# A transformer block with a mixture of experts: the router of the first 1536 tokens moved into the attention, the last 512 tokens prepared beside 16 expert tiles

## The reference

```python
h = _layernorm(x, axis=-1) * (1 + ca) + sa
x = x + ga * attention(h)         # 16 query heads of 64, 4 key/value heads, rotary, causal, fp32
h = _layernorm(x, axis=-1) * (1 + cb) + sb
x = x + gb * experts(h)           # 8 experts of 128 -> 512 -> 128, two per token

def experts(x):
    router_logits = x @ gate
    routing_weights, selected = jax.lax.top_k(router_logits, 2)
    routing_weights = jax.nn.softmax(routing_weights, axis=-1)
    out_of_expert = (silu(x @ w1[e]) * (x @ w3[e])) @ w2[e]
    return sum over the two selected experts of routing_weight * out_of_expert
```

## Time and profile before

| | us |
|---|---|
| three runs without a profile: median (lowest to highest) | 1238.19 (1237.99 to 1241.21) |
| the profiled execution, its own time | 1241.08 |
| its span | 1238.9 |
| TensorE busy in the span | 1088.2 (88%) |
| DVE busy | 854.7 (69%) |
| ScalarE busy | 540.0 (44%) |
| POOL busy | 603.7 (49%) |

### The profile page before, as it was taken

The page is one execution under the profiler, slowest core; times in us unless marked ns, Lnnn a source line. Parts: engine busy times, 40 slices in busy tenths (PEclk is TensorE's granted clock), DMA queues, the critical chain, the costliest instruction groups (busy, mean ns, idle before and its releaser), DMA issues.

```text
span 1238.9 us, 16497 instructions
## 1 busy us (share of the span) xinstructions
PE 1088.2 (88%) x5698; PEld 657.5 (53%) x5698; DVE 854.7 (69%) x1680; ACT 540.0 (44%) x1149; POOL 603.7 (49%) x649
## 2 busy tenths in 40 slices
PE   3589999999999999999999999999999973039993
PEld 2355555554565655455655554555565533029993
DVE  3647878777778786868787867778786658305553
ACT  2344544544445445454454545454544433014441
POOL 2733645645346565346446735445545233734441
PEclk9689999999999999999999999999999996559997
DMA  8000000000000000000000000000000006121104
GB/s 233 1 1 1 1 2 1 1 1 1 1 1 1 1 1 1 1 1 2 1 1 1 1 1 1 1 1 1 1 1 1 1 1 203 46 60 51 48 23 117
DMA packets 31921, 25.08 MB, mean 20 GB/s; under 512 B 8432, under 2 KB 26992, under 8 KB 31840
## 3 DMA queue, kind: packets, MB, share of 16 engines
q1 hardware_dynamic: 22272, 16.94, 4.6%
q0 software_dynamic: 2272, 4.72, 1.1%
q10 hardware_dynamic: 7296, 2.36, 0.8%
HBM read 15.62 MB, written 8.40 MB: 19 GB/s over the span
## 4 chain that ended last, share of the span: by engine, by line
PE 74%; DVE 12%; POOL 5%; issue 3%; DMA 2%; ACT 2%; ACTq 1%; SPq 0%; POOLq 0%; DVEq 0%
PE PS L1205 19%; PE PS L1159 12%; PE PS L1187 11%; PE PS L1189 9%; PE PS L1270 4%; POOL sent L614 3%; PE PS L1135 3%; PE PS L1224 3%; PE PS L1289 2%; DVE part_max L885 2%; PE PS L1172 2%; PE PS L1142 2%; PE PS L1215 2%; DVE full L901 2%; PE PS L1162 1%
## 5 line engine op out<-in xcount | busy, mean ns | idle before, releaser
L885 DVE TENSOR_REDUCE part_max<-PS 128x1 f32<-128x512 f32 (+2 forms) x576 | 340.3, 618 | 134.0 <-PE PS L1159 111.8
L692 ACT ACTIVATE full<-PS 128x512 f32<-128x512 f32 x384 | 223.5, 599 | 198.2 <-PE PS L1189 186.1
L1187 PE MATMUL PS<-rounded 128*128 128x512 f32 (+3 forms) x640 | 271.9, 425 | 5.9 <-ACT diag L701 2.4
L1159 PE MATMUL PS<-rounded 128*128 128x512 f32 (+3 forms) x640 | 250.1, 417 | 2.4 <-DVE V L866 1.3
L561 POOL TENSOR_TENSOR full<-full 128x512 f32<-128x512 f32 x128 | 164.4, 1315 | 155.5 <-PE PS L1205 154.5
L1189 PE MATMUL PS<-rounded 128*128 128x512 f32 (+3 forms) x640 | 233.5, 365 | 0.0
L701 ACT ACTIVATE diag<-PS 128x512 f32<-128x512 f32 (+3 forms) x256 | 111.4, 441 | 216.3 <-PE PS L1192 186.3
L589 POOL TENSOR_TENSOR rot_cos<-qkv_sb,cos_sb 128x320 f32<-128x320 f32 x64 | 60.3, 942 | 276.3 <-DVE qkv_sb L863 274.0
L1159 PEld LDWEIGHTS PS<-rounded 128*128 128x128 f32 x640 | 119.8, 193 | 139.0 <-DVE part_max L885 62.2
L1205 PE MATMUL PS<-full,V 128*64 128x512 f32 x768 | 190.0, 605 | 0.0
L1187 PEld LDWEIGHTS PS<-rounded 128*128 128x128 f32 x640 | 122.9, 192 | 80.8 <-ACT diag L701 27.0
(11 more groups left out here) (153 smaller groups left out, 1481.9 us busy)
## 6 DMA issues: line engine op xcount, KB each, us to landing
full<-in_L_ffn_experts_w_dram SPq DMA_DIRECT2D x16, 256.0 KB, 6.9
sent<-full SPq DMA_DIRECT2D x1, 2574.0 KB, 18.9
full<-sent SPq DMA_DIRECT2D x9, 264.0 KB, 2.9
full<-made SPq DMA_DIRECT2D x8, 256.0 KB, 5.1
out_dram<-XA SPq DMA_DIRECT2D x4, 256.0 KB, 2.8
made<-attnT,back_to POOLq DMA_INDIRECT x39, 2.2
wqkv<-in_L_attn_Wq_dram ACTq DMA_DIRECT2D x1, 512.0 KB, 4.4
bqkv<-in_L_attn_bq_dram ACTq DMA_DIRECT2D x1, 512.0 KB, 9.8
```

The lines of the kernel that those rows point to most:

```text
L692: nc.scalar.activation(full[:, k % QUADS, r, :], PS[:, bank, :], ACT.Exp).then_inc(probs_ready, 1)
L885: nc.vector.reduce_max(part_max[:, t, b:b + 1], PS[:, bank, 0:width], AX.X).then_inc(ring_dve, 1)
L1159: last = nc.tensor.matmul(PS[:, bank, 0:w], QT[:, ch % 2, h, t * P:(t + 1) * P], KT[:, 0, keys:keys + w], start=True, stop=not last_bank)
L1187: nc.tensor.matmul(o, KT[:, 0, keys:keys + P], QT[:, ch % 2, h, q0:BANK], start=True, stop=False)
```

## The change

It splits the tokens into a first batch of 12 tiles (1536 tokens, EARLY) and a second of 4 tiles.

* First batch: statistics, normalisation, turning, router, ranks, counts and slots become steps of `n.order` in the last two pairs (30 and 31). The first batch is placed in whole expert tiles first, and what an expert has beyond full tiles goes behind them. At least 16 tiles are then full (EARLY_SLOTS). POOL's 24 sends stand in the walk too. Three of the eight subtractions of the weights' rounding are steps on DVE, three run on POOL after the walk, two on DVE ahead of the last `rowsum`.
* The sums of pair 29 and the third `out` come earlier in the last group.
* Second batch: `out` of the last chunk, norm, router, ranks, counts, slots stand in the expert loop at the tiles 0 to 10 (`late(k)`), the 8 sends at tile 10. Quad 4, the first that needs them, is turned at tile 15.
* There is one more tile of slots: 40 in place of 39.
* `hidden_out` moves from DVE to ScalarE, `y_out` from ScalarE to DVE, where it also applies the gate. The eight multiplications of w2 on POOL go away.
* Until tile 10 `down` has one PSUM bank (5), since the second (7) serves the late steps.
* Memory is laid out anew, and SP's loads have new waits.

```diff
-    SLOT_TILES = 2 * TILES + NX - 1
-    SLOT_QUADS, Y_ROWS = 3, 8
+    SLOT_TILES = 2 * TILES + NX
+    SLOT_QUADS, Y_ROWS = 4, 8
+    EARLY, EARLY_LOWS = TILES - TB, 3
+    EARLY_SLOTS = (2 * EARLY * P - NX * (P - 1) + P - 1) // P // TB * TB
...
-    last_pair = [place(diag_steps(7), 8.01, 8.38), place(tail_steps(7), 8.4, 9.0)]
+    last_pair = [
+        place(diag_steps(5), 6.05, 6.1), place(tail_steps(5), 6.15, 6.5),
+        place([("ln_stats", 0)], 6.54, 6.55), place([("ln_scale", 0)], 6.59, 6.6),
+        place([("ln_turn", r) for r in range(CHUNKS - 1)], 6.66, 6.72),
+        place([("router", 0)], 6.76, 6.78), place([("count", 0)], 6.9, 6.92),
+        place([("send", t) for t in range(EARLY)], 6.95, 7.9), place([("weights", e) for e in range(EARLY_LOWS)], 7.2, 7.6),
+        place(diag_steps(7), 8.01, 8.38), place(tail_steps(7)[:-1], 8.4, 9.0),
+    ]
...
+            if k == EARLY_SLOTS - 1:
+                return EARLY_SLOTS // TB
+            q = k // TB + 1
+            return q if k % TB == 1 and q < QUADS_OF_SLOTS and q != EARLY_SLOTS // TB else None
...
+            return LATE_BANK if k > LATE_SEND and k % 2 else 5
...
+        LATE_OUT, LATE_TURN, LATE_ROUTER, LATE_COUNT, LATE_SEND = 0, 3, 4, 7, 10
...
+            for e in range(FIRST_RAW):
+                load_raw(e)
+            sp.wait_ge(slots_ready, 1)
+            sp.wait_ge(owners_ready, 1)
+            for e in range(FIRST_RAW, NEXT_RAW):
+                load_raw(e)
+            sp.wait_ge(scattered, 2 * EARLY * 16)
+            for e in range(NEXT_RAW, NX):
+                load_raw(e)
+            sp.wait_ge(pv_done, n.number["pv"])
+            sp.wait_ge(diag_added, n.number["diagsum"] // 2)
+            sp.dma_start(w2_sb, w2.rearrange("x (t p) e -> p x t e", p=P)).then_inc(ld_w2, 16)
...
+            for q in range(QUADS_OF_SLOTS):
+                if q >= SLOT_QUADS:
+                    sp.wait_ge(x_turned, q - SLOT_QUADS + 1)
+                    sp.wait_ge(back_ready, q - SLOT_QUADS + 1)
+                if q == EARLY_SLOTS // TB:
+                    sp.wait_ge(scattered, 2 * TILES * 16)
+                fetch(q)
...
+                elif kind == "ln_stats":
+                    dve.wait_ge(ring_dve, n.emptied(("out", GROUPS * CHUNKS - 2))[1])
+                    tile_stats(XA, range(EARLY))
+                    variance(range(EARLY))
...
+                    tables()
+                elif kind == "ln_scale":
+                    normalise(XA, rows_early, range(EARLY), 2)
+                elif kind == "router":
+                    bank = ring_wait(x)
+                    ranks(0, PS[:, bank, 0:EARLY * NX], ring_dve)
+                elif kind == "count":
+                    weights(0)
+                    bank = ring_wait(x)
+                    early_places(PS[:, bank])
...
+                nc.vector.scalar_tensor_tensor(out=y_rows[:, k % Y_ROWS, :], in0=PS[:, y_bank(k), 0:E],
+                                               scalar=weight_of[:, k:k + 1], in1=gates[:, 1, :],
+                                               op0=ALU.mult, op1=ALU.mult).then_inc(y_copied, 1)
...
+            pe.wait_ge(attn_ready, n.at["norm", LAST - 1] + 1)
+            turn_rows(0)
             pe.wait_ge(owners_ready, 1)
-            pe.wait_ge(w13_ready, NX)
-            pe.wait_ge(w2_ready, 1)
-            turn_rows(0)
+            pe.wait_ge(low_pool, len(POOL_LOWS))
+            pe.wait_ge(low_dve, EARLY_LOWS + len(DVE_LOWS))
+            pe.wait_ge(ld_w2, 16)
```

More of the change, by code:

```diff
@@ L98, in weight @@
                 "diagsum": 3.3, "quadsum": 0.01, "sum": 2.8, "rowsum": 12.6, "norm": 2.8, "modulation": 0.0,
-                "out": 8.0}[x[0]]
+                "out": 8.0, "ln_stats": 1.0, "ln_scale": 1.0, "ln_turn": 2.0, "router": 4.0, "count": 4.0, "send": 1.0,
+                "weights": 1.0}[x[0]]
     def maxima(J, m):
@@ new lines, in block_kernel @@
+        TABLES = [tables_of(lower[:, beats_at:hT_early_at]), tables_of(in_full(EARLY * NX * NX))]
+        small = carver(V[:, 0:2 * TB].rearrange("p i d -> p (i d)"))
+        ones16, earlier16 = small(P // 2).bitcast(BF16), small(P // 2).bitcast(BF16)
+        numbers, owner_of, weight_of, other, upto = (small(SLOT_TILES), small(SLOT_TILES), small(SLOT_TILES),
+                                                     small(SLOT_TILES), small(NX, NX))
+        load_of, full_tiles, until, limit, first, jump, left, spill, until_late = (small(NX) for _ in range(9))
@@ L632, in _ @@
                     send_back(k - 2)
-                if k % TB == 1 and k // TB + 1 < QUADS_OF_SLOTS:
-                    split_rows(k // TB + 1)
+                if k == LATE_SEND:
+                    for t in range(EARLY, TILES):
+                        send(t)
+                if quad_turn(k) is not None:
+                    split_rows(quad_turn(k))
             send_back(SLOT_TILES - 2)
@@ L1068, in _ @@
                   .then_inc(hidden_ready, 1)
-                if k >= 1:
-                    hidden_out(k - 1)
-                if k % TB == 1 and k // TB + 1 < QUADS_OF_SLOTS:
-                    addresses(k // TB + 1)
-            hidden_out(SLOT_TILES - 1)
+                if k >= 2:
+                    y_out(k - 2)
+                late(k)
+                if quad_turn(k) is not None:
+                    addresses(quad_turn(k))
+            y_out(SLOT_TILES - 2)
+            y_out(SLOT_TILES - 1)
             def of_chunk(t, ch):
```

657 lines of the change are left out of this document (397 added, 260 removed).

## The result

The changed kernel takes **1221.54 us** (median of four runs, 1218.72 to 1223.55) against 1238.12 of the kernel before on the same chip: ratio 0.985, 95% interval 0.983 to 0.986. The forecast was 1217, the range 1191 to 1232. The profiled execution took 1220.18, with a span of 1218.3 us in place of 1238.9.

What follows compares the result with a forecast made beforehand. The bound was TensorE's 93 us hole between attention and experts, filled by routing, sends and fetch. Quad 0 earlier -39.8, extra tile +2.8, late steps +15.7 gave -21.3: 1219.8 profiled, 1217 us as median, range 1191 to 1232.

Steps and rivals of the forecast that it cites:

- step 4: Expert loop: one more tile, +2.8 us, and the second batch's late steps, +15.7 us (bounds 8 and 28).
- Step 1: First batch's routing in the attention's last pairs: 11 us of TensorE delay, slots at 996.5 us (bounds 985 and 1003).
- (a): Attention: ScalarE waits for the statistics amid the exponentials, leaving TensorE idle for 4 us.
- (b): Attention: three groups of transposes wait for the 12 normalisations, slowed beside POOL's work: 4 us.
- Step 2: POOL's 24 early sends with eight `poolsum` between: all landed at 1047.2 us (bounds 1038 and 1062).
- 9 sends slowed, +9: POOL's early sends: DVE work with both inputs in SBUF slows nine of them by 1.0 us each.
- Step 3: SP's weight loads, then the fetch: quad 0 lands behind w2 at 1061.7 us, 39.8 us earlier than before.
- Tiles 0 to 3: Loop start: `out` at the low clock, and square root and two table loads ahead of a silu: together +3.9 us.
- the full VectorE queue: Loop: late ranks and slots in DVE's queue hold back the next tile's product by up to 3.3 us: +1 us.
- The rules weighed: ScalarE table switches: 1.28 us or the skill's 2.66 (sum 1222); shared SBUF port: pair 31 some 3 us later by rule.
- Overlap in name only: Rival, loop: DVE's late tables hold back sends, TensorE waits for quad 4, clock falls: +12 us, 1225 to 1233, chance 0.14.
- POOL is locked out all along: Rival: any DVE work slows sends and `poolsum`: +28 us, 1245; slower or no change had chance 0.10.

Runs made afterwards that it cites:

- fetch_first: Changed kernel with quad 0 fetched ahead of the w2 load and TensorE waiting for w2 only at tile 2: 1217.70 us, ratio 0.985.
- sends_again: Changed kernel with the eight indirect sends of the last 512 tokens issued a second time at tile 34: 1230.18 us, ratio 0.991.
- lows_on_dve: Changed kernel with GpSimd's three weight subtractions (experts 3 to 5) moved to VectorE: 1221.12 us, ratio 0.986.

## Why the prediction was right, and where it was not

**The measure.** Against the profiled executions the sum was -21.3 and came out as -20.9 (1241.08 to 1220.18). The medians differ by 16.6 only. I took 2.9 us off because before's profiled execution was so much above its median, and with it expected after's to be above its own; it was 1.4 below. That the sum is met to 0.4 us is luck: its two large parts were off by 6.9 and 7.6 us in opposite directions. What held is the mechanism of the gain: quad 0 lands 46.7 us earlier, since the routing of its tokens lies beside the attention. What is missing is a term of step 4, below.

**Step 1, slots at 996.5: 995.35.** `quadsum` of pair 30 was to start at 984.4 and started at 984.04. The parts, from the timelines of VectorE, ScalarE and TensorE:

```profile
960.78 2.41 DVE L865 BATCH_NORM_STATS2 stats<-XA 128x6 f32<-128x128 f32 x12
...
966.39 3.17 DVE L881 TENSOR_SCALAR lower<-XA,moments,rstd 128x128 f32<-128x128 f32 x12
...
984.04 4.90 DVE L1000 TENSOR_TENSOR full<-full 128x512 f32<-128x512 f32 x8 [0.21 <-DVE store L990]
...
995.17 0.18 DVE L1125 CAST slot_of<-wo_sb 128x24 uint32<-128x24 f32 x1
```

```profile
964.37 0.21 ACT L724 ACTIVATE rstd<-moments 128x12 f32<-128x12 f32 x1 [4.93 <-DVE moments L873]
```

```profile
966.54 0.79 PE L1368 MATMUL PS<-store 128*128 128x512 f32 x1 [5.10 <-ACT full L764]
```

(a) TensorE is idle for 5.10 us behind ScalarE's wait for the statistics, where I took 4. It then runs at the low clock until 972 us (granted 0.55 from 966.5 on), which I had at nothing. That is some 2.5 us more, an estimate: 0.45 of the 5.5 us of work in that stretch. (b) The 12 normalisations take 3.17, as alone in the earlier trace rows, because `poolsum` of pair 30 started only at 971.04: the contention of this step did not occur. TensorE did not stand there either, but `quadsum` came 10.6 us later all the same. What takes the place of those 4 us is mostly the low clock of (a), and the transposes and router products, which take 3.7 us on TensorE (3 predicted, with the counts); VectorE waits 2.5 us for a product of the maxima and 2.4 for the router. The sum was right, its make-up was not.

**Step 2, landed at 1047.2: 1041.05.** The term that failed is "9 sends slowed, +9". The group of the 24 sends (count, busy us, mean ns, then idle time before):

```profile
L662 POOL DMA_INDIRECT sent<-lower,slot_of x24 | 27.3, 1138 | 25.3 <-DVE slot_of L1125 18.4 <-issue 6.9
```

24 times 178 ns above 960 are 4.3 us, not 9. Thirteen sends were slowed, more than the nine I charged, but by 0.3 each and the worst by 0.8. The 1.97 of the earlier trace rows was no exception in the trace of before; three sends in a row took it beside VectorE's subtractions, which ran on to 1063.5 us and not to 1061.2:

```profile
1056.68 1.97 POOL L614 DMA_INDIRECT sent<-full,slot_of  x1 [0.30 <-issue]
1058.95 1.96 POOL L614 DMA_INDIRECT sent<-full,slot_of  x1 [0.30 <-issue]
1061.21 1.97 POOL L614 DMA_INDIRECT sent<-full,slot_of  x1 [0.31 <-issue]
```

Those subtractions are 128x1024 and come one behind the other, 1.15 us each. Most of what VectorE does beside the sends here are additions of 128x512, 0.4 to 0.7 us each. The slowest send of the changed kernel, 1.79 us at 1011.04, stands beside a subtraction of 128x1024 (1.23 us at 1010.77). So I priced short instructions like long ones; that the length decides is my reading, no run isolates it. `poolsum` took 9.89 (10.0 predicted). The rest is the earlier slots.

**Step 3, SP.** From the last landing to quad 0 it took 13.7 us (14.5 predicted). But the sentence that the code has no way to a quad 0 ahead of w2 was about the code as it stood. `fetch_first` shows that one line and a wait at tile 2 bring the start of the loop 3.5 to 5 us forward.

**Step 4, the loop: 15.7 predicted, 23.3 measured.** Tiles 0 to 3 took 4.6 (3.9), the table loads at tile 5 together with the clock behind them 3.9 (2), TensorE's late transposes, router and counts 1.8 (1.2), the full VectorE queue 0.9 (1). Quad 4 took 5.6 (7.6): its turning was open as predicted, and the wait for its rows did not happen, because the stall had already made TensorE late. **The stall at 13, 7.3 us, is missing.** The step was 7.6 us short; the other misses above nearly cancel. The step said of the late sends only when they land. It counted POOL's own time and asked who waits for the rows, not what the sends do to engines that share nothing with them in the program.

**The rules weighed.** Both table loads of tile 5 take 1.28 us in this trace, and the silu starts 0.01 behind its load. By the rule of the Trainium skill (ScalarE: Activation LUTs, What ACT_TABLE_LOAD costs) the sum was 1222. The trace disagrees with the rule here too. 1222 is nearer to the median than 1217, but not by that mechanism: the missing 7 us lie where no table is loaded. The lockout of `poolsum` beside `quadsum` that no row of before could show occurred: VectorE's eight `quadsum` of pair 31 took 9.57 in place of 4.9 us. They were on no path, since w2 and the fetch came later.

**The rivals.** "Overlap in name only" named the right place and the wrong cause: the late sends took 0.96 each, none was slowed, and what stood was TensorE, ahead of quad 4 and not waiting for its rows. "POOL is locked out all along" did not come: lockouts were found, but on VectorE mostly.

**What was to show it.** Quad 0 landed at 1054.78, a little ahead of the 1055 to 1068 forecast and behind the 1050 that would have refuted it. POOL released `quadsum` of pair 31, as forecast. From the first to the last gate_up it took 134.3 us, 21 beyond 40 tiles of 2.83, under the limit of 28. TensorE did not wait for quad 4's rows at tile 15, which the forecast had it do; the clock around it was under 1, as forecast (0.59 from 1128 to 1131 us). Of sends near 2 us there is one, of 1.79.

## What to carry to other kernels

Indirect DMAs from GpSimd beside a TensorE loop are not free even when nobody waits for them: eight in a row cost TensorE 7 to 10 us here in all three places tried (tiles 7, 10 and 34), eight plain ones nothing. So put them where TensorE idles anyway, and when you price a moved step, look at what ran beside it before: the kernel before had its 32 sends in the hole, where TensorE had nothing to lose. And when a load is needed a few tiles into a loop, wait for it there, not at the loop's entrance.

## What was not expected of the hardware

* By the modelled ends of the matmuls, TensorE's results reach VectorE and ScalarE 3.3, 4.2 and 8.5 us late in the rows above while GpSimd issues indirect DMAs every 1.26 us, and 4.2, 5.2 and 9.6 us late in `sends_again`. Each of eight such sends cost 0.7 to 1.2 us of the loop. Plain DMAs on the same queue do nothing of the kind, and neither register reads on TensorE nor the place in the loop decide it. The Trainium skill (SBUF — State Buffer, SBUF: two separate sides) says that on the engines' side TensorE waits for no other engine; by what path the sends hold it up no run here tells, and it stays open.
* In the attention, 18 indirect sends in the same rhythm did much less. From `quadsum` of pair 30 to the last product it took 42.7 us (984.04 to 1026.73) against 39.2 before (973.41 to 1012.64): 3.5 us for the sends and all other new work there. Why the loop is hit and the attention is not is open too.
* A VectorE add of 0.69 us took 7.71 beside three GpSimd subtractions in a row, and 0.69 again once they were gone (`lows_on_dve`).
